# A perceiver layer in float32: the stores of turned context move from the sync engine's queue to ScalarE's

## What is computed

```python
q_hk    = (layernorm(x) @ Wq.T).reshape(b, s, H, K)
q_big   = einsum('bshk,hkq->bshq', q_hk, w_kc_q)
kv_rope = kv_c * cos + rotate_half(kv_c) * sin        # the turned context
q_r     = einsum('bshq,hqr->bhsr', q_big, W_qr)
k_r     = einsum('bld,hdr->bhlr', kv_rope, W_kr)
attn    = softmax(einsum('bhsr,bhlr->bhsl', q_r, k_r))
ctx_c   = einsum('bhsl,bld->bhsd', attn, kv_rope)
out     = einsum('bhsd,hkd->bshk', ctx_c, w_kc_kv).reshape(b, s, H * K) @ Wo.T
```

## Time and profile before

| what | value |
| --- | --- |
| time, median of 3 executions | 1071.37 us (1069.65 to 1073.22) |
| profiled execution: its time | 1073.56 us |
| profiled execution: its span | 1071.7 us |
| TensorE busy, share of the span | 972.2 us, 91% |
| TensorE's granted clock, mean | 0.967 of full speed |
| ScalarE busy | 413.5 us, 39% |
| GpSimd busy | 416.1 us, 39% |
| stores of turned context | 28 of 256 KB, median 3.6 us from issue to landing |

### The profile page before, as it was taken

One profiled execution on the slowest core, in us unless ns is written; L12 is line 12 of the kernel. 1 busy time (PEld: TensorE's weight loads), 2 busy tenths in 40 slices (PEclk: granted clock), 3 DMA queues, 4 the chain that ended last, 5 costly groups with the idle time before them and its releaser, 6 DMA issues. The chain is left out here.

```text
span 1071.7 us, 15903 instructions
## 1 busy us (share of the span) xinstructions
PE 972.2 (91%) x5479; PEld 815.3 (76%) x5479; DVE 566.9 (53%) x1067; ACT 413.5 (39%) x954; POOL 416.1 (39%) x444
## 2 busy tenths in 40 slices
PE   5898976899999983799999999899999999999988
PEld 4666645777777762688888898786778899999977
DVE  6233358888888837444554432324986433333335
ACT  2333347766676626423422224452333122222101
POOL 0787854333433306000000120405732879892041
PEclk9999988999999996899999999998999999999999
DMA  6776722111111102322241003412021856671143
GB/s 201 214 242 210 220 78 79 35 36 40 38 32 40 30 1 79 118 79 79 83 136 37 20 21 92 156 31 93 2 81 51 269 194 214 204 227 61 43 138 98
DMA packets 79001, 109.89 MB, mean 103 GB/s; under 512 B 14224, under 2 KB 46992, under 8 KB 78928
## 3 DMA queue, kind: packets, MB, share of 16 engines
q1 hardware_dynamic: 70320, 89.52, 26.6%
q10 hardware_dynamic: 6048, 11.01, 3.1%
q0 software_dynamic: 2560, 8.39, 2.4%
HBM read 83.13 MB, written 25.77 MB: 102 GB/s over the span
## 5 line engine op out<-in xcount | busy, mean ns | idle before, releaser
L43 PE MATMUL psum<-second_xT_hi,mlp_w_hi 128*128 128x512 f32 x272 | 108.1, 397 | 8.5 <-DVE mix_wo_lo L1556 5.7
L44 PE MATMUL psum<-second_xT_lo,mlp_w_hi 128*128 128x512 f32 x272 | 107.4, 395 | 0.0
L45 PE MATMUL psum<-second_xT_hi,mlp_w_lo 128*128 128x512 f32 x272 | 107.2, 394 | 0.0
L1070 POOL TENSOR_TENSOR all_x<-all_x,mlp_raw 128x512 f32<-128x512 f32 x8 | 10.0, 1291 | 185.4 <-DVE all_x L1568 185.4
L2081 ACT ACTIVATE moe_s<-psum 128x352 f32<-128x352 f32 x39 | 18.1, 465 | 156.6 <-PE psum L45 140.8
L43 PEld LDWEIGHTS psum<-second_xT_hi,mlp_w_hi 128*128 128x128 f32 x272 | 52.0, 191 | 20.9 <-DVE mix_wo_lo L1556 6.1
L2147 DVE TENSOR_TENSOR moe_hT_lo<-psum,moe_hT_hi 128x384 fp32r<-128x384 f32 x39 | 21.7, 558 | 83.0 <-ACT moe_hT_hi L2087 83.0
L1525 ACT ACTIVATE mlp_s<-psum,mlp_side 128x512 f32<-128x512 f32 x32 | 21.9, 683 | 110.1 <-PE psum L45 110.1
L1568 DVE TENSOR_TENSOR all_x<-all_x,psum 128x512 f32<-128x512 f32 x64 | 43.9, 687 | 33.1 <-PE psum L45 32.3
L43 PE MATMUL psum<-moe_w_hi,moe_tT_hi 128*128 x184 | 61.3, 333 | 0.0
L742 POOL TENSOR_TENSOR first_xT_hi<-q_rows,first_xT_hi 128x256 fp32r<-128x256 f32 x28 | 20.7, 739 | 104.4 <-ACT first_xT_hi L831 104.4
(11 more groups left out here) (326 smaller groups left out, 2926.5 us busy)
## 6 DMA issues: line engine op xcount, KB each, us to landing
mlp_raw<-in_fc SPq DMA_DIRECT2D x16, 512.0 KB, 4.8
kv_all<-all_x SPq DMA_DIRECT2D x28, 256.0 KB, 3.6
far_raw<-in_eg SPq DMA_DIRECT2D x10, 704.0 KB
far_raw<-in_eu SPq DMA_DIRECT2D x10, 704.0 KB
slot_rows<-mix_W SPq DMA_DIRECT2D x23, 256.0 KB, 5.8
slot_out<-far_rows ACTq DMA_DIRECT2D x23, 256.0 KB, 2.2
far_raw<-in_ed SPq DMA_DIRECT2D x10, 512.0 KB
far_rows<-slot_rows ACTq DMA_DIRECT2D x19, 256.0 KB, 2.7
```

Of the source, the lines that this page charges most:

```text
L43: e.matmul(out, hi_l, hi_r, start=first, stop=False)
L44: e.matmul(out, hi_l, lo_r, start=False, stop=False)
L45: return e.matmul(out, lo_l, hi_r, start=False, stop=last)
L1070: pool.tensor_tensor(g["x"][:, t, :], g["x"][:, t, :], b2, ALU.add).then_inc(x_plus, 1)
```

## The change

`store_context` goes from SP's stream to ScalarE's. ScalarE issues the store of a batch directly after its own copy of that batch's columns, with one wait for that copy. SP's stream keeps the loads, in the same order as before. Nothing else changes; the number of stores, their size and their semaphores stay.

```diff
@@ SP @@
-            def store_context(b):
-                u = b % KVB
-                sp.wait_ge(rot, b + 1)
-                sp.wait_ge(kvT_ok, b + 1)
-                sp.dma_start(d["kv_all"][b], kvx[:, u, :, :, :].rearrange("p a c k -> p (a c k)")).then_inc(kv_out[u], 16)
-
             def contexts(b):
                 if b + RAW < B:
                     load_context(b + RAW)
                 if b % 2 == 1 and b + 3 < B:
                     load_tails((b + 3) // 2)
-                if 0 <= b - 2 < B - KEPT:
-                    store_context(b - 2)
@@ ScalarE @@
+            def store_context(b):
+                u = b % KVB
+                act.wait_ge(kvT_ok, b + 1)
+                act.dma_start(d["kv_all"][b], kvx[:, u, :, :, :].rearrange("p a c k -> p (a c k)")).then_inc(kv_out[u], 16)
+
@@ for p in range(NP) @@
                 if p + 1 < NP:
                     context_columns(BPP * p)
+                    store_context(BPP * p)
                 keep_features(p, 1)
                 if p + 1 < NP:
                     context_columns(BPP * p + 1)
+                    store_context(BPP * p + 1)
                     keep_a(p + 1)
...
                 context_columns(BPP * p + 2)
+                if p + 1 < NP:
+                    store_context(BPP * p + 2)
                 keep_queries(p, 1)
...
                 context_columns(BPP * p + 3)
+                if p + 1 < NP:
+                    store_context(BPP * p + 3)
```

## The result

| | before | changed |
| --- | --- | --- |
| median | 1073.38 us (1069.65 to 1083.84, 20 runs) | 1065.26 us (1059.51 to 1074.88, 20 runs) |
| profiled execution, span | 1071.7 us | 1071.9 us |

The ratio is 0.9916, with a 95% interval of 0.989 to 0.9942: about 9 us faster, and 6.2 at the least. A second set of runs of the same two kernels gave 0.9895 (0.9852 to 0.9937). The forecast was 1063.0 us in a range of 1058.5 to 1069. But the profiled execution of the changed kernel is no shorter than the one of before; at 1073.99 us it was one of the two longest of its twenty. That has to be explained too, and the heads come first.

A forecast was written before the change was run, and what follows sets the result against it. TensorE was taken to set the heads' pace, with GpSimd close and held by late stores. 8.9 us in six pairs plus 1.7 at the end gave 10.6, from 1073.56 to 1063.0 us; range 1058.5 to 1069.

The forecast's parts named there:

- The bound, read from "issue" waits: Heads: GpSimd's 17.8 us idle ahead of L358, in 17 places, are waits for late stores, until TensorE waits for GpSimd.
- 8.9 us in six pairs: Heads, first features of pair 1 to pair 7: 91.99 us falls to 6 x 13.85 = 83.1, saving 8.9 us.
- 1.7 us at the end: Pair 7, the heads' end: batch 30's transposition no longer waits 1.73 us for GpSimd; the last batch's wait counts nothing.
- Everything behind the heads: 0: After the heads: everything starts earlier by the same amount and does the same work, charged 0.
- ScalarE's cost: 0: Heads: 28 issues and waits at 0.5 us each, 14 us, lie where ScalarE waits for TensorE anyhow; charged 0.
- Transfers: Heads: DMA engines' share rises from 0.77 to 0.82, landings may grow from 3.9 to 5.5 us; charged 0.
- The time in hand: Heads: 2.7 us between store 3's early landing and batch 7's earliest start, to cover longer landings.
- The rule: Skill's rule on shared DMA engines: stores land no faster, saving some 0.4 us of sync engine; prediction adds time before issue.
- Only issue time is saved: Rival, heads: stores leave early but land when they did, every wait stays, 1073.6 us; chance 0.08.
- Raw loads become the limit: Rival, heads: raw loads become GpSimd's limit, about half of the 10.6 us goes, 1068.3 us; chance 0.12.
- ScalarE is held: Rival, heads: issues hold ScalarE, making the place behind copy 5 2.5 us late per pair, 1080.5 us; chance 0.05.
- the slow pair: Heads, the pair of 18.20 us against 14.7: said to more than explain the 2.2 us above the median, and to go.

The follow-up runs named there:

- early sync version: Kernel before, stores still on the sync engine's queue, but each batch's store issued ahead of the raw load and tail rows; ratio to before 0.9889, again 0.9882.
- two copies of lag: Changed kernel, but ScalarE issues each store after the copy of columns two batches later; ratio to the kernel before 1.0066.
- four-issue version: Changed kernel with each store cut into four DMAs of 32 partitions, 112 issues instead of 28; ratio to the kernel before 0.9962.

## Why the prediction was right

**The bound, read from "issue" waits.** Right, and shown: 17.8 us of idle time without a releaser were waits for stores; with early issue, on either queue, or with one more buffer, TensorE's pace is the same (83.67, 83.11, 83.45 us). With five buffers and the old order some of these waits stay, and they end again with a store's landing.

**8.9 us in six pairs.** The measured difference is 91.99 - 83.67 = 8.3 us, and 94.15 - 83.40 = 10.8 in the second pair of profiles. The pace of 13.85 us, put together from four pieces of different pairs, was exact: four of the six pairs take 13.82 to 13.85. The other two take 14.17 and 14.14. TensorE's second queries wait there 0.68 and 0.65 us for VectorE's copy of the first ones, which stands behind an operation (`heads_k_lo`, L605) that took 0.83 and 0.79 us instead of 0.28. Why it did stays open; the first such pair also appears in the second profile of the early sync version, so it is not ScalarE's issues.

**1.7 us at the end.** From ScalarE's first features of pair 7 to the last transposition it was 149.9 - 137.8 = 12.1 us and is 139.3 - 129.8 = 9.5: 2.6 us; in the second pair of profiles 12.3 and 9.6. The step that was too small is the last batch's wait for GpSimd, which I had counted as nothing. In the second profile of before, batches 30 and 31 waited 1.90 and 0.82 us, which is the whole difference, at a clock of 1.00. In the first they waited 1.73 and 0.25, and the clock fell as well (0.87 in rows 2, 0.54 from 148 to 150 us, where batch 31 was turned).

**Everything behind the heads: 0.** Nearly. The stretch from the heads' end to the attention's first output took 71.5 and 69.3 us before, 74.0 and 72.3 after. Some 2 to 3 us are given back there in these profiles. The mean granted clock of that stretch was 0.89 and 0.95 before, 0.86 and 0.91 after, and for the same work TensorE was busy 54.7 and 51.3 us before, 56.9 and 54.9 after, so most of it is the clock. It does not hang on the early end of the heads alone: with two copies of lag the heads ended at 155.5 us, later than before, and the stretch took 72.4 us at a clock of 0.86. What lowers the clock there stays open. Of 10.6 and 13.4 us gained in the heads (last transposition at 153.3 and 139.9 in the second profiles), 8.6 and 10.2 are left at the first scatter, and 8.1 between the medians.

**ScalarE's cost: 0.** Right: 0.33 us an issue, and the wait for its own copy 0.02 to 0.04 us behind the copy's end, where I had allowed up to 0.38 and taken 0.17. Its room was read correctly as well: the four-issue version overran it.

**Transfers.** The share of the DMA engines rose to 0.87 and 0.88, where 0.82 was worked out, and landings from 3.6 to 4.3 us (3.9 in the second profile). The time in hand covered this: store 3 left at 43.97 and landed 4.7 us later, at 48.7, and batch 7 started at 51.04, 2.4 us behind it, where 2.7 had been worked out.

**The rule.** The Trainium skill, page "DMA: Bandwidth & Descriptors", section "Issuing engines are not separate DMA queues", says that transfers of all issuing engines run on the same 16 DMA engines, so that spreading them saves issue time only. The landings here agree: 3.8 and 4.0 us at the median with the stores early on the sync engine, 4.3 and 3.9 with them on ScalarE. What was gained was the time before the issue, and one queue in a better order gives it too.

**The rivals.** "Only issue time is saved" is refuted by the pairs. "Raw loads become the limit" is half true: they are what GpSimd waits for now (3.7 us), but TensorE sets the pace. "ScalarE is held" did not happen with 28 issues; with 112 it took half the gain.

**The check on the sum.** 1063.0 us against a median of 1065.26: the sum started from one execution at 1073.56, close to the later median of 1073.38, so the shift of 2.2 us towards the first three runs was rightly not made. I had argued that the slow pair explained those 2.2 us; it does not, since it came back. Some luck is in the closeness: the heads ended 10.6 us earlier, the very sum, but it came from 0.6 us less in the pairs, 0.9 more at the end and a start 0.3 later, and in the second profiles it was 13.4; then 2 to 3 us that were put at nothing went the other way.

## What to carry to other kernels

In a queue that is worked off in order, ask of each transfer what stands ahead of it and for whom that waits: a store behind the waits of loads that belong to later steps is late by those steps, and it can hold the very engine it waits for. Such a loop shows as idle time without a named releaser on the engine that refills the buffer; check it by adding the landing time to the issue. Then compare the free time of the buffer with the engine's own pace: moving the issue earlier in the same queue, another queue, or one more buffer were worth the same here, and the choice goes by who has room for the issue.

## What the runs showed of the hardware

- Four DMA issues in a row on ScalarE cost more than four times one: 1.74 to 2.98 us against 4 x 0.33 (median of one 0.44, longest 1.65), for parts of 64 KB.
- ScalarE's issue behind a wait for its own copy starts 0.02 to 0.04 us after the copy's end. What the wait does cost is the overlap: with a lag of two copies, where the issue waits for an older copy, it starts together with the copy ahead of it in the stream, at 48.22 both:

```profile
48.22 0.38 ACT L537 ACTIVATE all_x<-psum 128x256 f32<-128x256 f32 x1 [0.97 <-PE psum L490]
48.22 0.33 ACTq L543 DMA_DIRECT2D kv_all<-all_x  x1
```

- Executions of one program lay up to 15 us apart (1059.51 to 1074.88), and one such difference, the 8.8 us at the experts, stood in a place far from the change, with TensorE idle for 5.4 us and its granted clock at 0.90 instead of 1.00. Two profiles of each kernel, cut into the same stretches of work, told this apart; the spans alone did not.
